# A mixture of experts: weights of experts 1 to 7 split ahead of time and kept in DRAM, and output parts made in three steps

## The reference

```python
h = jax.nn.relu(x @ rW1 + rb1)
h = jax.nn.relu(h @ rW2 + rb2)
scales = jax.nn.softmax(h @ rW3 + rb3, axis=-1)
topk_scales, topk_experts = jax.lax.top_k(scales, k)
...
dispatched = dispatched.at[e_flat, b_idx, pos_c].set(jnp.where(keep[..., None], x_rep, 0.0), mode='drop')
hh = jax.nn.relu(jnp.einsum('ebnc,ech->ebnh', dispatched, eW1) + eb1[:, None, None, :])
eout = jnp.einsum('ebnh,ehc->ebnc', hh, eW2) + eb2[:, None, None, :]
gathered = eout[e_flat, b_idx, pos_c]
gathered = jnp.where(keep[..., None], gathered, 0.0).reshape(B, T, k, C)
out = jnp.sum(topk_scales[..., None] * gathered, axis=2)
```

## Time and profile before

| | us |
|---|---|
| three runs | 2481.61, 2486.73, 2487.48 |
| median | 2486.73 |
| the profiled execution | 2483.57 |
| its span in the trace | 2482.0 |
| PE busy in the span | 2360.9 |
| DVE busy | 1176.5 |
| ACT busy | 1074.0 |
| POOL busy | 179.0 |
| router, about | 1751 to 2192 |
| experts, about | 2215 to 2439 |
| final products begin | 2453.5 |

### The profile page before, as it was taken

One profiled execution on the slowest core, in us unless ns is written; L12 is line 12 of the kernel. 1 busy time (PEld: TensorE's weight loads), 2 busy tenths in 40 slices (PEclk: granted clock), 3 DMA queues, 4 the chain that ended last, 5 costly groups with the idle time before them and its releaser, 6 DMA issues.

```text
span 2482.0 us, 51076 instructions
## 1 busy us (share of the span) xinstructions
PE 2360.9 (95%) x18944; PEld 1552.3 (63%) x18963; DVE 1176.5 (47%) x2305; ACT 1074.0 (43%) x2053; POOL 179.0 (7%) x256
## 2 busy tenths in 40 slices
PE   6999999998999799999999999999799999989997
PEld 2444688886878444444445888888344444457776
DVE  5553455446888453332322433333544445355553
ACT  3553445443666342332323333332345444457671
POOL 0000000003343000000000000000000000002123
PEclk9999999998999899999999999999899999989997
DMA  3330011102333231121110000001211111016663
GB/s 120 102 102 34 31 52 51 34 17 65 85 91 81 65 128 43 43 76 43 43 43 26 31 30 13 13 13 47 69 35 34 34 34 34 0 38 107 93 106 102
DMA packets 152205, 136.91 MB, mean 55 GB/s; under 512 B 93128, under 2 KB 135304, under 8 KB 145144
## 3 DMA queue, kind: packets, MB, share of 16 engines
q1 hardware_dynamic: 137804, 76.78, 12.0%
q0 software_dynamic: 10928, 55.60, 7.9%
q10 hardware_dynamic: 3324, 2.51, 0.3%
HBM read 90.80 MB, written 34.60 MB: 51 GB/s over the span
## 4 chain that ended last, share of the span: by engine, by line
PE 83%; ACT 5%; SPq 4%; DVE 4%; issue 2%; DMA 2%; POOL 0%; DVEq 0%; ACTq 0%; POOLq 0%
PE ps L694 31%; PE ps L711 25%; PE ps L955 13%; PE ps L1077 4%; PE ps L944 3%; PE ps L1065 3%; SPq L506 1%; DMA arena<-in_x 1%; SPq L505 1%; ACT arena L1225 1%; ACT misc L1226 1%; SPq L392 1%; PE ps L1101 1%; SPq L581 1%; PE ps L969 1%
## 5 line engine op out<-in xcount | busy, mean ns | idle before, releaser
L694 PE MATMUL ps<-xh,arena 128*128 (+1 forms) x5376 | 909.1, 312 | 18.4 <-DVE xh L1471 10.3
L711 PE MATMUL ps<-misc,arena 128*128 128x256 f16 (+1 forms) x4128 | 726.0, 312 | 8.9 <-DVE misc L1541 5.5
L694 PEld LDWEIGHTS ps<-xh,arena 128*128 (+1 forms) x5376 | 527.7, 98 | 290.5 <-issue 27.2
L711 PEld LDWEIGHTS ps<-misc,arena 128*128 (+1 forms) x4128 | 403.2, 98 | 222.0 <-issue 7.8
L1545 DVE SCALAR_TENSOR_TENSOR misc<-ps,misc 128x256 f16<-128x256 f32 (+1 forms) x480 | 255.0, 532 | 542.5 <-ACT misc L1158 541.7
L1158 ACT ACTIVATE misc<-ps 128x256 f16<-128x256 f32 (+1 forms) x480 | 225.0, 469 | 553.0 <-PE ps L694 553.0
L955 PE MATMUL ps<-arena 128*128 128x512 f16 x1536 | 336.7, 379 | 0.0
L955 PEld LDWEIGHTS ps<-arena 128*128 128x128 f16 x1536 | 148.2, 98 | 173.4
L1808 DVE TENSOR_TENSOR arena<-misc,arena 128x512 f16<-128x512 f32 x128 | 88.6, 692 | 229.4 <-ACT arena L1293 229.4
L1539 DVE TENSOR_TENSOR arena<-ps,misc 128x256 f32<-128x256 f32 (+1 forms) x208 | 105.2, 506 | 143.9 <-ACT misc L1154 143.1
L1154 ACT ACTIVATE misc<-ps 128x256 f32<-128x256 f32 (+1 forms) x208 | 93.5, 450 | 162.4 <-PE ps L694 161.7
(11 more groups left out here) (243 smaller groups left out, 2008.8 us busy)
## 6 DMA issues: line engine op xcount, KB each, us to landing
wstage<-in_m_w POOLq DMA_DIRECT2D x16, 1024.0 KB, 5.2
arena<-src_d SPq DMA_DIRECT2D x64, 256.0 KB, 3.7
src_d<-misc SPq DMA_DIRECT2D x24, 512.0 KB, 3.1
wstage<-in_c_wi POOLq DMA_DIRECT2D x6, 1024.0 KB, 5.5
wstage<-in_r_w POOLq DMA_DIRECT2D x5, 1024.0 KB, 5.3
cexp_d<-misc SPq DMA_DIRECT2D x18, 256.0 KB, 2.5
src_d<-misc SPq DMA_DIRECT2D x18, 256.0 KB, 2.5
cshare_d<-misc SPq DMA_DIRECT2D x8, 512.0 KB, 3.1
```

Of the source, the lines that this page charges most:

```text
L694: last = mm(ps[:, bank, col:col + p.n], weight(off, half, g, wp, k * F + f * 128), xh[:, xp, k, ds(start, p.n)], start=(k == 0 and n == 0) ...
L711: last = mm(ps[:, 4 + 2 * half + m, 0:p.n], weight(place[0], half, 2 if p.gated else 1, wp, f * D + m * 128), hid[:, st % 4, hp, 0:p.n], s ...
```

## The change

1. In the router, steps 9 to 15 of every chunk each convert one quarter of a matrix (128x512): ACT the high part (`piece_high`), DVE the low part (`piece_low`), both into one of two small buffers `piece`. That is 7 pieces in each of 8 chunks, 56 for the 14 matrices of experts 1 to 7. POOL stores each piece into a DRAM tensor `parts_d` and fetches the next matrix behind every fourth piece. ACT waits for the store of piece n-2 before it writes piece n. ACT's loop over chunks 1 to 6 is written out.
2. During the experts nothing is converted. The finished parts of expert 1 are loaded by SP behind the router, those of expert e+1 by ACT at steps 4 and 5 of expert e, 1 MB each, straight into the slots. TensorE waits for these loads at an expert's first product.
3. The three operations of a tile's output stand in three successive steps: for tiles 0 to 2 DVE's sum at steps 8 to 10, ACT's high part at 9 to 11, DVE's low part at 10 to 12; for tiles 3 and 4 at steps 1 and 2, 2 and 3, 3 and 4 of the next expert. The buffer `ev` alternates over all tiles.
4. POOL loads the first two quarters of x1 right behind the last piece, no longer in expert 6.

```diff
+        piece = misc[:, 5440:6464].bitcast(F16).rearrange("p (u h n) -> p u h n", u=2, h=2)
...
+        parts_d = scratch("parts_d", [2 * (NE - 1), 128, 2, MAT], F16)
...
         for e in range(1, NE):
-            wait = (s["l_mm"], 8) if e == 1 else (s["m_out"], 2 * (e - 1))
-            loads += [(a["m_w1"][e], MOE_W[e % 2][0], SW, wait), (a["m_w2"][e], MOE_W[e % 2][1], SW, wait)]
+            loads += [(a["m_w1"][e], None, SW, None), (a["m_w2"][e], None, SW, None)]
...
+            for n in range(8 * (NE - 1)):
+                pool.wait_ge(s["mw_lo"], n + 1)
+                pool.dma_start(parts_d[n // 4, :, :, (n % 4) * 512:(n % 4 + 1) * 512], piece[:, n % 2]
+                               ).then_inc(s[f"mw_st{n % 2}"], 16)
+                if n % 4 == 3 and FIRST_MOE + 2 + n // 4 < len(loads):
+                    fetch(FIRST_MOE + 2 + n // 4)
+            x1_back(0)
+            x1_back(1)
             for e in range(NE):
-                for i in range(FIRST_MOE + 2 * e + 2, min(FIRST_MOE + 2 * e + 4, len(loads))):
-                    fetch(i)
-                if e == NE - 2:
-                    pool.wait_ge(s["w_ready"], len(loads))
-                    x1_back(0)
-                    x1_back(1)
                 for t in range(5):
...
+            for u in range(2):
+                sp.wait_ge(s[f"mw_st{u}"], 64 * (NE - 1))
+            sp.wait_ge(s["l_mm"], 8)
+            for w in range(2):
+                slot = MOE_W[1][w]
+                sp.dma_start(arena[:, slot * SLOT:(slot + 1) * SLOT], parts_d[w].rearrange("p h n -> p (h n)")
+                             ).then_inc(s["mw_in1"], 16)
...
-                    pe.wait_ge(s["w_ready"], e * 2 + FIRST_MOE)
+                    if e == 0:
+                        pe.wait_ge(s["w_ready"], FIRST_MOE)
+                    else:
+                        pe.wait_ge(s[f"mw_in{e % 2}"], 32 * ((e + 1) // 2))
...
+            def piece_high(n):
+                i, q = FIRST_MOE + n // 4, n % 4
+                if q == 0:
+                    act.wait_ge(s[f"w_in{i % 2}"], 16 * (i // 2 + 1))
+                if n >= 2:
+                    act.wait_ge(s[f"mw_st{n % 2}"], 16 * (n // 2))
+                fn(piece[:, n % 2, 0, :], wstage[:, i % 2, q * 512:(q + 1) * 512], ACT.Copy, scale=SW).then_inc(s["w_hi"], 1)
...
+                    if st >= 9:
+                        piece_high(c * 7 + st - 9)
             z_parts(0, 0)
             z_parts(1, 1)
             router(0, True, True)
-            with act.Fori(1, 7) as c:
-                router(c, False, True)
-            router(7, False, False)
+            for c in range(1, 8):
+                router(c, False, c < 7)
...
-            def expert_weight_high(e, w, h):
-                i = FIRST_MOE + 2 * e + w
-                slot, cols = loads[i][1], slice(h * (MAT // 2), (h + 1) * (MAT // 2))
-                if h == 0:
-                    act.wait_ge(s[f"w_in{i % 2}"], 16 * (i // 2 + 1))
-                    act.wait_ge(*loads[i][3])
-                fn(w16(slot, 0, h * (MAT // 2), MAT // 2), wstage[:, i % 2, cols], ACT.Copy, scale=SW
-                   ).then_inc(s["w_hi"], 1)
...
-                    fn(eo[:, t, 0, :], ev[:, t % 2, :], ACT.Copy).then_inc(s["eo_hi"], 1)
+                    fn(eo[:, t, 0, :], ev[:, (e * 5 + t) % 2, :], ACT.Copy).then_inc(s["eo_hi"], 1)
+            def expert_weights(e, w):
+                slot = MOE_W[e % 2][w]
+                act.wait_ge(s["m_out"], 2 * (e - 1))
+                act.dma_start(arena[:, slot * SLOT:(slot + 1) * SLOT], parts_d[2 * (e - 1) + w].rearrange("p h n -> p (h n)")
+                              ).then_inc(s[f"mw_in{e % 2}"], 16)
             def expert(e, fresh=False):
                 if fresh:
                     act.wait_ge(s["consts"], 1)
                 for st in range(16):
                     ehidden(e, st)
-                    if st in (1, 2) and not fresh:
-                        eout(e - 1, 1, (2 + st,))
-                    if st in (8, 9, 10):
-                        eout(e, 0, (st - 8,))
-                    if st in (2, 3, 5, 6) and e + 1 < NE:
-                        expert_weight_high(e, int(st >= 5), int(st in (3, 6)))
+                    if st in (4, 5) and not fresh and e + 1 < NE:
+                        expert_weights(e + 1, st - 4)
+                    if st in (2, 3) and not fresh:
+                        eout(e - 1, 1, (1 + st,))
+                    if st in (9, 10, 11):
+                        eout(e, 0, (st - 9,))
...
+            def piece_low(n):
+                i, q = FIRST_MOE + n // 4, n % 4
+                dve.wait_ge(s["w_hi"], 4 * i + q + 1)
+                last = v.scalar_tensor_tensor(piece[:, n % 2, 1, :], wstage[:, i % 2, q * 512:(q + 1) * 512], SW, piece[:, n % 2, 0, :],
+                                              ALU.mult, ALU.subtract)
+                last.then_inc(s["mw_lo"], 1)
+                if q == 3:
+                    dve.wait_ge(s["mw_lo"], n + 1)
+                    dve.sem_inc(s["w_ready"], 1)
...
+                    if st >= 9:
+                        piece_low(c * 7 + st - 9)
...
-            def eout(e, half, tiles=None):
-                for t in (tiles or TILES[half]):
-                    dve.wait_ge(s["m_out"], e * 2 + (half + 1))
-                    if t >= 2:
-                        dve.wait_ge(s["eo_lo"], e * 5 + (t - 1))
-                    elif t == 0 and not (isinstance(e, int) and e == 0):
-                        dve.wait_ge(s["eo_lo"], e * 5)
-                    v.scalar_tensor_tensor(ev[:, t % 2, :], ps[:, 3 + t, 0:D], SEO / (SR * SW), misc[:, ds(e * D + 4608, D)],
-                                           ALU.mult, ALU.add).then_inc(s["ev"], 1)
-                    dve.wait_ge(s["eo_hi"], e * 5 + (t + 1))
-                    v.tensor_tensor(eo[:, t, 1, :], ev[:, t % 2, :], eo[:, t, 0, :], ALU.subtract).then_inc(s["eo_lo"], 1)
-            def expert(e, par, fresh=False, lastone=False):
+            def eout_sum(e, t):
+                dve.wait_ge(s["m_out"], e * 2 + (1 if t < 3 else 2))
+                if e * 5 + t >= 2:
+                    dve.wait_ge(s["eo_lo"], e * 5 + t - 1)
+                v.scalar_tensor_tensor(ev[:, (e * 5 + t) % 2, :], ps[:, 3 + t, 0:D], SEO / (SR * SW), misc[:, ds(e * D + 4608, D)],
+                                       ALU.mult, ALU.add).then_inc(s["ev"], 1)
+            def eout_low(e, t):
+                dve.wait_ge(s["eo_hi"], e * 5 + (t + 1))
+                v.tensor_tensor(eo[:, t, 1, :], ev[:, (e * 5 + t) % 2, :], eo[:, t, 0, :], ALU.subtract).then_inc(s["eo_lo"], 1)
+            def expert(e, fresh=False):
                 for st in range(16):
                     n = len(TILES[st // FC]) * 128
                     dve.wait_ge(s["m_hi"], e * 16 + (st + 1))
...
                                     hid[:, st % 4, 0, 0:n], ALU.subtract).then_inc(s["m_lo"], 1)
                     if fresh and st == 3:
                         bias_scaled()
+                    if st in (3, 4) and not fresh:
+                        eout_low(e - 1, st)
+                    if st in (10, 11, 12):
+                        eout_low(e, st - 10)
                     if st in (1, 2) and not fresh:
-                        eout(e - 1, 1, (2 + st,))
+                        eout_sum(e - 1, 2 + st)
                     if st in (8, 9, 10):
-                        eout(e, 0, (st - 8,))
-                    if st in (4, 5, 6, 7) and not lastone:
-                        w, h = divmod(st - 4, 2)
-                        slot, cols = MOE_W[1 - par][w], slice(h * (MAT // 2), (h + 1) * (MAT // 2))
-                        dve.wait_ge(s["w_hi"], 4 * FIRST_MOE + e * 4 + (2 * w + h + 1))
-                        last = v.scalar_tensor_tensor(w16(slot, 1, h * (MAT // 2), MAT // 2),
-                                                      wstage[:, (FIRST_MOE + w) % 2, cols], SW,
-                                                      w16(slot, 0, h * (MAT // 2), MAT // 2), ALU.mult, ALU.subtract)
-                        if h:
-                            last.then_inc(s["w_ready"], 1)
-            expert(0, 0, fresh=True)
-            for e in range(1, NE - 1):
-                expert(e, e % 2)
-            expert(NE - 1, 1, lastone=True)
-            eout(NE - 1, 1)
+                        eout_sum(e, st - 8)
+            expert(0, fresh=True)
+            for e in range(1, NE):
+                expert(e)
+            for t in TILES[1]:
+                eout_sum(NE - 1, t)
+            for t in TILES[1]:
+                eout_low(NE - 1, t)
```

1 line of the change is left out of this document (added).

## The result

The changed kernel takes 2528.66 us (median of five runs, 2516.85 to 2533.13) against 2485.97 us before (median of five runs). The ratio is 1.017, 95% interval 1.0141 to 1.0198. The forecast was 2476 with a range of 2469 to 2484, so it was wrong in sign, and the range missed the time by 45 us. The profiled execution is the fastest of the five, 2516.85 us with a span of 2514.9, which is 32.9 us more than the 2482.0 of before.

The account below looks back on a forecast made before the run. TensorE was taken to bound the expert stage, SP's last stores the end. Seven experts at 1.65 us (-11.55) plus 1.07 gave -10.5, other terms 0: from 2486.73 to 2476.2, forecast 2476, range 2469 to 2484.

Parts of the forecast that it names:

- the budget of the loads: Experts: the second 1 MB weight load has 14.9 us from issue to need; taken to land in time, cost 0.
- weights late: Rival, 8%: expert weights land after 14.9 us, each further us costs six; 2490 at 17.2 us, 2524 at 22.8.
- The steps: Experts: three-step output parts remove all three TensorE waits for DVE per expert, 1.65 us each, 11.55 us for experts 0 to 6.
- the later low part: Expert 7, tile 0: DVE's low part (L1852) falls behind step 10's subtraction, 1.07 us later, added to the time.
- The router: Router: 56 added conversion pieces and their POOL stores stay off TensorE's path, no TensorE wait there; cost 0.
- The end: Last products wait for SP's 28 stores of expert 7: end is its tile 0 plus 24.7 us, whatever TensorE does.
- the stall only moves: Rival, 15%: ACT is full in expert steps 9 to 11, half of 1.65 us stays, gain 4.7 us, time 2482.
- the store of a piece holds ACT: Rival, 5%: in the router ACT waits for piece stores landing in 10.3 us, 23 us more, time 2499.

## Why the prediction was wrong

**The step that failed** is the budget of the loads, and in it this sentence: "I take in time, since the pair is now issued after the stores of tiles 3 and 4 and before those of tile 0." It was read off step numbers. ACT's loads stand at steps 4 and 5 and DVE's low parts, which release the stores, at steps 3 and 4; but ACT reaches its step 4 when DVE is at its step 3, and in the timeline the two fall 0.05 us apart. The load met the stores it was said to follow. The order was not the whole error, though: with the loads two steps later, when they did follow these stores, the second of a pair still landed 19.0 us after its issue on average. What the step had wrong is how long a 1 MB load takes beside stores into neighbouring partitions, and so it put the waits for loads at 0. Landing took 18.2 to 21.9 us for the second load of each pair, and the late loads cost 38.9 us. The budget itself was about right: 16.0 us by the trace (need at 2267.36, issue at 2251.37), 14.9 forecast.

**The value chosen was the wrong end.** The text had 7.6 us and 14.0 to 17.2 us for a 1 MB load, and counted on the first ("Against it: 7.6"). But those weight loads were issued 15 and 18 us into an expert, the first of them into DMA engines that were nearly idle (in expert 2 a share of 0.05 from 2282.0 to 2284.7 us), and 7.6 is only their median. The row by line of the kernel before has their spread:

```profile
L429 POOL DMA_DIRECT2D wstage<-in_m_w x12: 531/541/560, 2227.5 to 2371.4; - x12
...
DMA to landing us min/median/max: 4.9/7.6/20.7
```

A weight load of 20.7 us was there to be seen. The 14.0 was measured beside expert stores, as here, and was the nearer row.

**The rival "weights late"** had the mechanism and 8%. Its price was too low: six waits of 4.2 us on average (20.2 less 16.0) make the 25.4 of the trace, but what comes behind them, the lower clock above all, adds another 13.5 us. The text had no term for that, though it knew the level of 0.50 from the earlier trace rows.

**The steps** were right: all 24 waits gone, experts 26.14 us apart where 26.2 was forecast, 11.8 us for seven experts where 11.55 was. SP's first store of expert 7 comes 2457.73 - 2455.31 = 2.42 us behind the sum, 2.4 forecast, so the later low part shifts it by 1.06 us, 1.07 forecast; the last products move by 0.7 only, since SP is through with its 28 stores 0.4 us sooner. In the run with the steps alone the gain came to 7.4 us in the medians, not 10.5; in its profile the experts began 1.6 us later than in that of before, and one expert lost 1.7. Over all profiles the first mark lies between 2231.4 and 2239.5 us, so 1.6 is within what varies from one to the next.

**The router** was right: the last piece of TensorE's work in it begins at 2192.5 in place of 2191.2 us. The text says that no TensorE wait is listed in the whole router; one is, of 2.1 us before that last piece, in both kernels alike. A piece store landed in 2.5 us at the median, as the row of the 256 KB store said, and ACT waited for one three times, 4.2 us in all, which reached nobody.

**The end** was right in kind (the last products start a fixed time behind tile 0 of expert 7) and missed 4.4 us behind them. With the loads in time the change comes to 2479.8 us (stores into DRAM) or 2482.0 (slots spread), and without them to 2478.3, not to 2476.

**The rivals "the stall only moves" and "the store of a piece holds ACT"** did not occur.

## What to carry to other kernels

Before a transfer is moved, list what else is in flight at the new moment, in times and not in step numbers, and take the landing from a row with the same neighbours. A stretch where the DMA engines' share is near 1 and the rate is a fraction of what they move elsewhere was here the sign of many stores into neighbouring partitions: try first to spread the destinations over partitions far apart, before anything is timed around them. And where the wait is on TensorE, price it with the products at the lower clock behind it: here 39 us for 25 us of waits.
